# Layer 0's routed experts: the down projection's two weight halves as one 512-column operand

## The reference

```
h = silu(x @ W1[e].T) * (x @ W3[e].T)          # 256 -> 176
routed += combine[t, e] * (h @ W2[e].T)        # 176 -> 256
```

## Time and profile before

| | us |
|---|---|
| median of 3 runs | 1327.85 (1324.62 to 1328.19) |
| the profiled execution | 1328.39 |
| its span | 1326.7 |
| the routed experts, from the first split of weights to the last scatter | 530.6 to 742.6 |
| first and last `result` on ACT | 549.3, 740.3 |

### The profile page before, as it was taken

How to read it: one execution, slowest core, us unless ns; L and a number is a source line. 1 busy time by engine, 2 the same in 40 slices (tenths; PEclk the granted TensorE clock), 3 DMA queues, 4 the chain that set the end, 5 groups by cost and what they waited for, 6 DMA issues and landing times. The chain is left out here.

```text
span 1326.7 us, 21239 instructions
## 1 busy us (share of the span) xinstructions
PE 987.1 (74%) x5454; PEld 815.5 (61%) x5454; DVE 786.5 (59%) x1887; ACT 601.8 (45%) x1594; POOL 483.3 (36%) x646
## 2 busy tenths in 40 slices
PE   5356799999977688679999325558497960999990
PEld 2245678888866466569899213336385750788870
DVE  3764698999956753654444167788356652333333
ACT  0244798999953353555555112225232211333330
POOL 2345365666631773124444233334142421000005
PEclk9678799999987879799999757789698985999995
DMA  5235533333314232653333331100151003001004
GB/s 191 65 133 183 140 97 89 93 93 87 81 44 152 96 128 89 209 172 121 114 114 120 131 122 64 63 1 1 56 178 60 28 32 106 22 25 33 24 21 131
DMA packets 111890, 123.09 MB, mean 93 GB/s; under 512 B 46792, under 2 KB 85320, under 8 KB 111552
## 3 DMA queue, kind: packets, MB, share of 16 engines
q1 hardware_dynamic: 103408, 99.07, 25.3%
q0 software_dynamic: 8400, 23.01, 4.8%
HBM read 77.72 MB, written 44.32 MB: 92 GB/s over the span
## 5 line engine op out<-in xcount | busy, mean ns | idle before, releaser
L662 ACT ACTIVATE PR<-PS,nmax 128x128 f32<-128x128 f32 (+3 forms) x256 | 135.7, 552 | 9.8 <-DVE nmax L703 8.6
L580 POOL TENSOR_SCALAR PR<-PR,rinv 128x128 f32<-128x128 f32 (+3 forms) x256 | 131.6, 533 | 0.0
L703 DVE TENSOR_REDUCE nmax<-PS 128x1 f32<-128x128 f32 (+3 forms) x256 | 113.9, 483 | 24.0 <-PE PS L606 18.7
L1297 POOL DMA_INDIRECT r_results<-r_y,r_to x79 | 75.8, 959 | 135.9 <-DVE r_to L1348 84.1
L711 DVE TENSOR_TENSOR PTlo<-PS,PThi 128x512 fp32r<-128x512 f32 (+1 forms) x192 | 103.3, 593 | 2.9 <-ACT PThi L672 2.9
L672 ACT ACTIVATE PThi<-PS 128x512 fp32r<-128x512 f32 (+1 forms) x192 | 96.7, 545 | 11.5 <-PE PS L618 11.5
L605 PE MATMUL PS<-K,Q 128*128 128x128 f32 (+3 forms) x256 | 84.7, 391 | 10.5 <-PEq L259 5.7
L618 PE MATMUL PS<-ident,PR 128*128 128x128 f32 x640 | 87.9, 284 | 3.3 <-DVE PTlo L711 2.7
L2145 POOL DMA_INDIRECT x_yg<-x_results,d_slots x16 | 18.0, 1125 | 196.9 <-DMA x_results<-x_y 192.4
L634 PE MATMUL PS<-PThi,V 128*128 128x512 f32 (+3 forms) x256 | 85.1, 345 | 4.0 <-DMA V<-v_parts 3.0
L2198 DVE TENSOR_TENSOR x_h<-PS,x_sg 128x256 f32<-128x256 f32 x68 | 28.9, 425 | 92.9 <-ACT x_sg L2167 92.9
(11 more groups left out here) (356 smaller groups left out, 3123.3 us busy)
## 6 DMA issues: line engine op xcount, KB each, us to landing
r_xg<-r_sorted SPq DMA_DIRECT2D x79, 129.0 KB, 2.1
r_wst<-in_routed SPq DMA_DIRECT2D x16, 608.0 KB, 4.8
K<-k_parts SPq DMA_DIRECT2D x128, 64.0 KB, 1.8
c_yg<-r_results SPq DMA_DIRECT2D x16, 512.0 KB
v_parts<-vp SPq DMA_DIRECT2D x4, 1024.0 KB, 5.0
Q<-q_parts SPq DMA_DIRECT2D x64, 64.0 KB, 1.8
Q<-q_parts SPq DMA_DIRECT2D x128, 32.0 KB, 1.7
V<-v_parts SPq DMA_DIRECT2D x64, 64.0 KB, 2.1
```

The costliest lines, as they stand in the source:

```text
L580: pool.tensor_scalar(PR[:, e % 4, i, 0:w], PR[:, e % 4, i, 0:w], rinv[:, e % 4, i:i + 1], 1.0, ALU.mult, ALU.mult).then_inc(norm_done, 1)
L662: act.activation(PR[:, e % 4, i, 0:w], k.PS[:, i, 0:w], ACT.Exp, bias=nmax[:, e % 4, i:i + 1], accum_out=rsum[:, e % 4, i:i + 1]).then_inc ...
L703: dve.tensor_reduce(nmax[:, e % 4, i:i + 1], k.PS[:, i, 0:P * (i + 1)], AX_X, ALU.max, negate=True).then_inc(max_done, 1)
L1297: pool.indirect_dma_start(out=d.results, out_offset=bass.IndirectOffsetOnAxis(ap=to[:, i % TO_LANES:i % TO_LANES + 1], axis=0), in_=y[:, i ...
```

## The change

The down weights of an expert get a tile of their own, `w2`, in which for each half of the inner width the 256 rounded columns and the 256 columns of the rest lie side by side. The product with the stationary rounded activations (`hhi`) is then one matmul of 512 columns, which gives hi x hi in the left 256 columns of PSUM and hi x lo in the right 256; the product lo x hi (`hlo` stationary) is added to the left columns by a matmul of 256 columns. So `down` has 4 matmuls instead of 6, with as many columns. Its order is `hhi`, `hlo` of the first half of the inner width, then `hlo`, `hhi` of the second.

The two halves in PSUM have to be added. ACT's `result` now takes the right half, times the row's weight, into a new tile `yr`, and DVE's new `result` makes `y` = left half times the row's weight plus `yr`. `y_done` comes from DVE now. DVE has its `result` ahead of its `split_h` in a step, and the wait for the lane of `y` has moved to it.

ACT and DVE split an expert's weights with two instructions each instead of one (704 and 512 columns), and DVE waits for both of ACT's. `xg` has 7 lanes instead of 8, so that `yr` finds room. In the diff the first `result` is ACT's, the second DVE's.

```
-X_LANES, Y_LANES, TO_LANES = 8, 3, 12
+X_LANES, Y_LANES, TO_LANES = 7, 3, 12
...
-        whi, wlo = sb("whi", [E, WR], F32R), sb("wlo", [E, WR], F32R)
+        whi, wlo = sb("whi", [E, DM * UP], F32R), sb("wlo", [E, DM * UP], F32R)
+        w2 = sb("w2", [E, 2, 2, D], F32R)
+        yr = sb("yr", [1, D])
...
-                    act.activation(whi[:, e, :], wst[:, e % W_LANES, :], ACT.Copy).then_inc(w_hi, 1)
+                    act.activation(whi[:, e, :], up, ACT.Copy).then_inc(w_hi, 1)
+                    act.activation(w2[:, e, :, 0, :], down.rearrange("p (f d) -> p f d", f=2), ACT.Copy).then_inc(w_hi, 1)
...
             def result(s):
                 act.wait_ge(y_ready, s + 1)
-                if s >= Y_LANES:
-                    act.wait_ge(d.y_out[s % Y_LANES], 16 * (s // Y_LANES))
-                act.activation(y[:, s % Y_LANES, :], PS_Y(s), ACT.Copy, scale=xg[:, s % X_LANES, D:D + 1]).then_inc(y_done, 1)
+                wait(act, y_done, s)
+                act.activation(yr[:, 0, :], PS_Y(s)[:, D:2 * D], ACT.Copy, scale=xg[:, s % X_LANES, D:D + 1]).then_inc(yr_done, 1)
...
-                    dve.wait_ge(w_hi, e + 1)
-                    dve.tensor_tensor(wlo[:, e, :], wst[:, e % W_LANES, :], f32(whi[:, e, :]), ALU.subtract).then_inc(w_done, 1)
+                    dve.wait_ge(w_hi, 2 * (e + 1))
+                    dve.tensor_tensor(wlo[:, e, :], up, f32(whi[:, e, :]), ALU.subtract).then_inc(w_done, 1)
+                    dve.tensor_tensor(w2[:, e, :, 1, :], down.rearrange("p (f d) -> p f d", f=2), f32(w2[:, e, :, 0, :]),
+                                      ALU.subtract).then_inc(w_done, 1)
...
-            steps((-3, split_weights), (-2, block_lo), (0, times), (2, split_h), (0, destination))
+            def result(s):
+                dve.wait_ge(yr_done, s + 1)
+                if s >= Y_LANES:
+                    dve.wait_ge(d.y_out[s % Y_LANES], 16 * (s // Y_LANES))
+                dve.scalar_tensor_tensor(out=y[:, s % Y_LANES, :], in0=PS_Y(s)[:, 0:D], scalar=xg[:, s % X_LANES, D:D + 1], in1=yr[:, 0, :],
+                                         op0=ALU.mult, op1=ALU.add).then_inc(y_done, 1)
+            steps((-3, split_weights), (-2, block_lo), (0, times), (3, result), (2, split_h), (0, destination))
...
-                    cols = slice(DM * UP + part * D, DM * UP + (part + 1) * D)
+                    both, narrow = slice(2 * part * D, 2 * (part + 1) * D), slice(2 * part * D, (2 * part + 1) * D)
-                    last = split3_moving(pe, PS_Y(s), hhi[:, s % 2, f], hlo[:, s % 2, f],
-                                         moving(whi, e, cols), moving(wlo, e, cols), part == 0, part == 1)
+                    if part == 1:
+                        pe.matmul(PS_Y(s)[:, 0:D], hlo[:, s % 2, f], moving(w2f, e, narrow), start=False, stop=False)
+                    last = pe.matmul(PS_Y(s), hhi[:, s % 2, f], moving(w2f, e, both), start=part == 0, stop=part == 1)
+                    if part == 0:
+                        pe.matmul(PS_Y(s)[:, 0:D], hlo[:, s % 2, f], moving(w2f, e, narrow), start=False, stop=False)
```

More of the change, by code:

```diff
@@ L1254, in routed_experts @@
             S("up_ready"), S("sg_done"), S("h_done"), S("hT_ready"), S("hhi_done"), S("hlo_done"))
-        y_ready, y_done, to_done, zeroed = S("y_ready"), S("y_done"), S("to_done"), S("zeroed")
+        y_ready, yr_done, y_done, to_done, zeroed = S("y_ready"), S("yr_done"), S("y_done"), S("to_done"), S("zeroed")
         block = c.enter_context(nc.Block())
         PS_UP, PS_X, PS_H, PS_Y = (lambda s: k.PS[:, s % 2, 0:UP], lambda s: k.PS[:, 2 + s % 2, 0:D],
-                                   lambda s: k.PS[:, 4 + s % 2, 0:2 * P], lambda s: k.PS[:, 6 + s % 2, 0:D])
+                                   lambda s: k.PS[:, 4 + s % 2, 0:2 * P], lambda s: k.PS[:, 6 + s % 2, :])
         def steps(*stages):
@@ L1269, in load_weights @@
                 if e < E:
-                    sp.wait_ge(w_done, e - W_LANES + 1)
+                    sp.wait_ge(w_done, 2 * (e - W_LANES + 1))
                     weights.load(sp, e)
@@ L1306, in split_weights @@
                     act.wait_ge(w_in[e % W_LANES], 16 * (e // W_LANES + 1))
-                    act.activation(whi[:, e, :], wst[:, e % W_LANES, :], ACT.Copy).then_inc(w_hi, 1)
+                    up, down = wst[:, e % W_LANES, 0:DM * UP], wst[:, e % W_LANES, DM * UP:]
+                    act.activation(whi[:, e, :], up, ACT.Copy).then_inc(w_hi, 1)
+                    act.activation(w2[:, e, :, 0, :], down.rearrange("p (f d) -> p f d", f=2), ACT.Copy).then_inc(w_hi, 1)
             def block_hi(s):
@@ L1363, in _ @@
             expert = {}
+            w2f = w2[:].rearrange("p e f a d -> p e (f a d)")
             pe.wait_ge(d.table_done, 2)
@@ L1374, in up @@
                 if s < E:
-                    pe.wait_ge(w_done, s + 1)
+                    pe.wait_ge(w_done, 2 * (s + 1))
                 expert[s] = pe.value_load(d.expert[0:1, s:s + 1], min_val=0, max_val=E - 1)
```

## The result

| | before | after |
|---|---|---|
| median, us (four runs each) | 1328.02 (1324.62 to 1329.08) | 1467.39 (1466.34 to 1469.74) |
| ratio | | 1.1058 (95%: 1.1032 to 1.1084) |
| span of the profiled execution | 1326.7 | 1468.0 |
| mean granted clock of PE | 0.861 | 0.841 |

The change makes the kernel 10.6% slower; the forecast was 1472 us, with a range of 1438 to 1504.

A forecast was written before the change was run, and what follows sets the result against it. The prediction took the loop through the `xg` lanes, already at the edge with eight, as the bound. On the profiled 1328.39 us, +1.5 +47.8 +88.1 +0.5 +6 = +143.9 gave 1472.3, as a median 1472; range 1438 to 1504.

The forecast's parts named there:

- Block 0's `y`: Start of the stage: DVE makes block 0's `y` behind the longer weight split of expert 6, +1.5 us.
- While weights arrive: Blocks 0 to 9: the loop through lane and weights spans one step, not two, 9.29 us a step, +47.8 us.
- Steady part: Blocks 9 to 73: the lane loop spans two steps, not three, 7.36 us a pair, +88.1 us.
- the clock: Steady part: PE's clock falls behind idle gaps in about one in eight steps, +6 us, between 0 and 64.
- Tail: After block 73: no block left to load, pace kept, the last `y` 0.45 us later, +0.5 us.
- `down`'s matmuls: `down` on PE: two matmuls and two loads fewer save 0.024 us a step, only where PE sets the pace.
- DVE's `result`: DVE's new instruction behind ACT's half: 0.45 us with 0.03 of hand-over, ends 0.33 and 0.6.
- 1: Rival: weights keep their two-step loop, so the 47.8 us fall away; 1424 us, chance 5%.
- 2: Rival: the steady part runs mostly at 1.2 GHz, +2 us a pair for 32 pairs; 1530 us, chance 5%.
- Rival 3: Lanes decide nothing; longer splits and DVE's place cost 6 us, DVE's order 4; 1338 us, chance 4%.
- 4: Rival: PE's pace decides all along, matmuls and loads saved give 1.9 us; 1326 us; 2% faster, 2% no change.
- signs: Expected in the trace, steady part: PE's busy share near 60%, waits for `r_xg` once in two steps, some 2 us each.

The follow-up runs named there:

- after_weights_first: The changed kernel with SP asking for blocks 3 ahead instead of 4 (AHEAD), so an expert's weights no longer stand behind the waiting load; 1424.63 us, ratio 1.0724.
- the last pair of kernels: Kernel before (1306.71 us) and changed kernel with DVE's `split_h` ahead of `result` (1308.9 us), both with `xg` lanes freed once `destination` copies the row's weight.
- after_8_lanes: The changed kernel with 8 lanes of `xg` again and no `yr`: ACT writes its half into `y`, DVE adds in place; 1351.56 us, ratio 1.0171.

## Why the prediction was right

Step by step, against the starts of `result`:

- *Block 0's `y`, +1.5:* -0.3. It ends at 549.41, not 549.76. But in this execution the whole stage began 1.4 us earlier (first split at 529.21, not 530.57), which the change has no part in. Counted from there, block 0's `y` takes 20.20 us instead of 19.19, +1.0.
- *While weights arrive, +47.8:* +47.9 (83.74 less 35.79 us). The mean load of weights over the nine steps, from issue to ACT, was 4.34 us (4.02 to 4.74), where 4.37 was taken. after_weights_first shows the cause as well as the size: with the queue's order undone 43 of it are gone.
- *Steady part, +88.1, and the clock, +6:* +90.2 together, so 4 us too much. Two parts of it were off, in opposite directions. Over the 61 loads between 642 and 864 the median from SP's issue to PE's `columns` is 2.15 us (lowest 2.02; the mean of 2.44 holds loads that landed while PE was still busy), not 2.6, and 3.54 from `columns` to DVE's `result`. With 1.27 from there to the issue the undisturbed pair is 6.96, and indeed the median of the pairs is 6.96. That is 222.7 us for 32 pairs, 12.8 less than the term. The other 15 us are in the disturbed pairs, 20 of the 63 counted from every block, at 7.6 to 10.0 us. The clock is a part of them, and it was put at 6. That the two errors nearly cancel is luck. The prediction says that the kernel before "confirms" the 2.6; it does not, since 2.6 had been fitted so that this kernel came out at 2.303, and held its disturbances already, spread over every load. With 2.15 the loop of the kernel before is 6.46 us for three steps, 2.15 a step beside a median step of 2.17: at the edge, as the prediction says, but most steps did not wait for it. The Trainium skill (DMA: Bandwidth & Descriptors, "Anatomy of one DMA") fits its figures to transfers that POOL issues, and these are issued by SP, which the prediction leaves out. Its 2.3 us, which I passed over as 10 us too low, is closer to the undisturbed load all the same; the row of this trace, 2.1, was closer still.
- *Tail, +0.5:* +4.4, the one term mis-sized by its mechanism. The prediction had the chain on DVE, at 2.3 us (it is 2.47), called it "hidden beneath 3.68", and said that "the tail keeps its pace". But the cover was the lane loop, and in the tail no block is left to load. Five blocks at its own 2.3 us a step, against 7.89 us in the kernel before, would have given +3.6.
- *`down`'s matmuls:* 0.024 a step was said; the last pair of kernels differs by 0.02, in one trace of each.
- *DVE's `result`:* 0.48 us, with 0.03 of hand-over 0.51, where 0.45 was taken.

The terms measured sum to -0.3 + 47.9 + 90.2 + 4.4 = 142.2; the spans differ by 141.3. Of the rivals, 1 would have shown 4 us a step while weights arrive, 2 a pair of 9.4 in the steady part (two of 63 took 10.0), 3 and 4 a PE that does not wait for `xg`. None describes what was seen. Rival 3's price for the rest of the change, 10 us, was half of what after_8_lanes shows, 22. Of the signs, two came out otherwise: PE was busy 73% of the steady part, not near 60%, though the prediction's own 2.06 us idle of 7.36 give 72%; and PE's waits for a block were 1.1 us each, not some 2.

## What to carry to other kernels

A ring of buffers is a loop: add up what lies between the last read of a buffer and the first use of its next content, divide by the steps that the ring spans, and compare with the step. It costs little while that quotient is below the step's own length. At equal length it costs what the late loads add (here 0.15 us a step, 2.303 against 2.156), and beyond it the loop sets the step, so that a buffer less costs its whole share (3.344). An engine that seems 97% busy can already stand at that edge. Before a buffer is given up, or one added, look at what holds it longest, and copy that bit aside.

## What the runs showed of the hardware

A late load costs twice: PE's clock can fall behind the gap, and then the loop's own matmuls are slower. Three rows of PE in the changed kernel, and the stretches around them (columns as in the earlier trace rows):

```profile
773.64 0.69 PE L1385 MATMUL PS<-ident,r_xg 128*128 128x128 f32 x2 [2.25 <-DMA r_xg<-r_sorted]
775.24 0.50 PE L2309 MATMUL PS<-r_whi,r_xhi 128*128 x1
778.12 0.63 PE L1385 MATMUL PS<-ident,r_xg 128*128 128x128 f32 x2
```

```profile
770.00:772.00 2.00, 1.39 (x9) 1.01 (x8) 0.74 (x3) 1.33 (x4) 0.96 (x1) 1.00 0.38 117
772.00:774.00 2.00, 0.36 (x2) 0.29 (x2) 0.81 (x3) 0.00 (x0) 0.83 (x1) 0.86 0.08 23
774.00:776.00 2.00, 1.84 (x7) 1.52 (x6) 0.00 (x0) 0.00 (x0) 0.13 (x1) 0.50 0.48 132
778.00:780.00 2.00, 2.00 (x8) 1.88 (x7) 0.88 (x3) 0.47 (x1) 0.00 (x0) 0.50 0.00 0
```

The load issued at 770.10 was used at 773.64, 3.54 us later instead of 2.15. PE had idled 2.25 us; the granted share went from 1.00 to 0.50 (2.4 to 1.2 GHz), and from this `columns` to DVE's `result` at 778.86 it took 5.22 instead of 3.54. So of the 3.1 us by which each of the two pairs around it is too long (10.0 instead of 6.96), 1.4 are the late load and 1.7 what ran slower behind it. Not every gap does it, and I found no rule in the rows: a gap of 2.10 us at 750.86 was followed by a fall too, one of 1.34 at 696.27 also, while those of 1.42 at 644.50, 1.34 at 651.38 and 1.91 at 866.65 left the share at 1.00. Why that load was late the trace does not show, and I did not try to part the clock's share of the 15 us above from the loads'.

The read of the expert's number stands in PE's program between `columns` and `up`. Between the two PE shows "issue" when it has just waited for a load, and none when it has not: from `columns` to `up` it took 1.02 us at 703.85, of which 0.57 was that idle time, and 0.53 in all at 654.25, where PE had not waited. That the read is what the "issue" stands for is taken from the program; the trace names nothing there. A buffer that comes late pays this on top.
